# Mixing the last rows of a relational basis on VectorE, with interleaved one-hots

## The reference

```
w = jnp.einsum('rb,bio->rio', att, basis)      # att (2, 30), basis (30, 512, 512)
...
msg = jnp.where((edge_type == 0)[:, None], msgs[0], msgs[1])
agg = jax.ops.segment_sum(msg, row, num_segments=x.shape[0])
```

## Time and profile before

| | us |
|---|---|
| median of three runs | 918.7 |
| the three runs | 917.99, 918.7, 922.83 |
| the profiled execution, its own time | 917.2 |
| span of its trace | 915.4 |
| TensorE busy | 882.8 (96%) |
| VectorE busy | 656.2 (72%) |
| ScalarE busy | 280.8 (31%) |
| mean granted clock of TensorE | 0.985 |

### The profile page before, as it was taken

How to read it: one execution, slowest core, us unless ns; L and a number is a source line. 1 busy time by engine, 2 the same in 40 slices (tenths; PEclk the granted TensorE clock), 3 DMA queues, 4 the chain that set the end, 5 groups by cost and what they waited for, 6 DMA issues and landing times.

```text
span 915.4 us, 12673 instructions
## 1 busy us (share of the span) xinstructions
PE 882.8 (96%) x4258; PEld 428.2 (47%) x4258; DVE 656.2 (72%) x1286; ACT 280.8 (31%) x431; POOL 87.9 (10%) x66
## 2 busy tenths in 40 slices
PE   7999999999959999899997999999999999999997
PEld 3555555554545444344443444444444444444443
DVE  6898978658987797998999988975324255552247
ACT  0333444637752116222312111114311221132221
POOL 1000111301220003021210000003200020020000
PEclk9999999999979999999998999999999999999999
DMA  8955665596435885788464655530131014322228
GB/s 275 352 168 165 183 188 191 149 238 198 155 95 157 200 236 150 208 207 204 128 150 108 155 141 161 139 91 1 35 81 23 12 47 139 82 62 41 47 60 237
DMA packets 134888, 129.50 MB, mean 141 GB/s; under 512 B 80687, under 2 KB 81156, under 8 KB 134826
## 3 DMA queue, kind: packets, MB, share of 16 engines
q10 hardware_dynamic: 96192, 60.25, 26.1%
q1 hardware_dynamic: 38634, 68.45, 24.9%
HBM read 97.80 MB, written 12.52 MB: 121 GB/s over the span
## 4 chain that ended last, share of the span: by engine, by line
PE 68%; DVE 15%; DMA 8%; ACT 4%; issue 2%; POOL 1%; DVEq 1%; ACTq 0%; SPq 0%
PE Dp L696 25%; PE Dp L666 24%; PE T L620 11%; PE Dp L572 6%; DVE acc L1262 4%; DMA stage<-in_basis 3%; DMA wst<-mixd 2%; DMA xr<-xres 2%; DVE Zraw L1373 1%; ACT W L1010 1%; DVE stt L1354 1%; ACT wst L863 1%; DVE w L1391 1%; PE T L666 1%; POOL Zraw L530 1%
## 5 line engine op out<-in xcount | busy, mean ns | idle before, releaser
L666 PE MATMUL Dp<-W,hT 128*128 128x512 f16 x792 | 175.7, 381 | 3.6 <-DMA hT<-S 3.6
L696 PE MATMUL Dp<-Zraw,A 128*128 128x512 f16 x800 | 173.0, 379 | 0.0
L1262 DVE SCALAR_TENSOR_TENSOR acc<-stage,att,acc 128x512 f32<-128x512 f32 x232 | 163.5, 770 | 4.3 <-DMA stage<-in_basis 4.3
L696 PE MATMUL Dp<-Zraw,AT 128*128 128x512 f16 x600 | 130.0, 379 | 0.0
L666 PEld LDWEIGHTS Dp<-W,hT 128*128 128x128 f16 x792 | 77.8, 98 | 96.6 <-DMA hT<-S 3.8
L696 PEld LDWEIGHTS Dp<-Zraw,A 128*128 128x128 f16 x800 | 78.2, 98 | 94.4
L696 PEld LDWEIGHTS Dp<-Zraw,AT 128*128 128x128 f16 x600 | 58.7, 98 | 70.8
L1140 DVE TENSOR_SCALAR Zraw<-hT,w 128x640 f16<-128x640 f16 (+1 forms) x209 | 85.9, 456 | 0.3
L1391 DVE SCALAR_TENSOR_TENSOR w<-Dp,aggc,S 128x512 f32<-128x512 f32 x40 | 29.9, 747 | 59.9 <-PE Dp L696 54.0
L962 ACT ACTIVATE Zraw<-Dp,zsc 128x512 f16<-128x512 f32 x46 | 29.4, 684 | 125.8 <-PE Dp L666 121.7
L620 PE MATMUL T<-stage,W 128*128 128x512 f32 x120 | 60.5, 627 | 5.5 <-DMA stage<-in_basis 5.5
(11 more groups left out here) (176 smaller groups left out, 950.4 us busy)
## 6 DMA issues: line engine op xcount, KB each, us to landing
stage<-in_basis SPq DMA_DIRECT2D x180, 256.0 KB, 2.9
Zraw<-in_basis SPq DMA_DIRECT2D x60, 256.0 KB, 3.1
xres<-w ACTq DMA_DIRECT2D x30, 256.0 KB, 2.3
xr<-xres ACTq DMA_DIRECT2D x30, 256.0 KB, 3.1
wst<-in_Wn ACTq DMA_DIRECT2D x4, 1024.0 KB, 5.6
wst<-in_Ws ACTq DMA_DIRECT2D x4, 1024.0 KB, 6.0
wst<-mixd ACTq DMA_DIRECT2D x4, 1024.0 KB, 6.0
wst<-in_root ACTq DMA_DIRECT2D x3, 1024.0 KB, 6.7
```

What stands on the lines that cost most here:

```text
L666: last = nc.tensor.matmul(dense_bank(u, t, m), turned[:, hp, k * P:(k + 1) * P], weights_of(u, m)[:, wp, k, :], start=(n == 0), stop=(n == ...
L696: last = nc.tensor.matmul(sum_bank(t), a[:, k, ds(t * P, P)], Z[:, r, h, k, :], start=(n == 0), stop=(n == count - 1))
L1262: last = v.scalar_tensor_tensor(part, stage[:, q, :], a, part, ALU.mult, ALU.add)
```

## The change

Seven of the eight groups stay on TensorE (`PE_GROUPS`), six of them spread over the 40 windows as 7, 7, 7, 7, 6, 6. The last 64 rows of both relations are mixed on VectorE: relation 0 on partitions 0 to 63, relation 1 on 64 to 127. For this the same 64 rows of each basis are loaded twice, once for each half, into two slots that lie in `bias`; the column of coefficients is `late_att`, the sum `late_sum` in `Zraw`. One such step, `late_mix`, stands at the end of each of the windows 8 to 37. On the SP queue the two loads of step b stand ahead of the matmul's loads of the same share, and wait until step b-2 is done (`l_done`).

The four low one-hots of a window are written interleaved: element 4k + c belongs to column k of chunk c. Their comparison takes a prepared table `iota_c` and four neighbouring values of `lo_h`, in place of a broadcast of one value along 128 columns. TensorE reads the stationary operand of these four chunks in steps of four elements.

```diff
-        GROUP_BLOCKS = [6, 6, 6, 6, 5, 5, 6]
+        GROUP_BLOCKS = [7, 7, 7, 7, 6, 6]
...
+            for r in range(REL):
+                sp.dma_start(late_att[r * 64:(r + 1) * 64, :], att1[2 + r:3 + r, :].broadcast_to([64, BASES])).then_inc(e_att, 16)
+
+            def load_late(b):
+
+                wait(sp, l_done, b - 1)
+                for r in range(REL):
+                    sp.dma_start(late_in[b % 2][r * 64:(r + 1) * 64, :],
+                                 basis1[PE_GROUPS, b // 2, b % 2 * 64:(b % 2 + 1) * 64, :]).then_inc(l_full[b % 2], 16)
+
+            at = PAIRS + 2 * NT
+            for b in range(BASES):
+                nxt = PAIRS + 2 * NT + (PAIRS * PE_GROUPS - PAIRS - 2 * NT) * (b + 1) // BASES
+                load_late(b)
+                load_mix(at, nxt)
+                at = nxt
+            sp.wait_ge(l_done, BASES)
...
+            pool.iota(iota_c, [[1, P], [0, 2 * FIXED]], base=0, channel_multiplier=0, **kw).then_inc(s_const, 1)
...
+                if isinstance(slot, int):
+                    n = 2 * FIXED
+                    four = slot // n * n
+                    low = oh_lo[:, four * P:(four + n) * P].rearrange("p (k c) -> p k c", c=n)[:, :, slot % n]
+                else:
+                    low = oh_lo[:, ds(slot * P, P)]
...
+            def late_out():
+
+                act.wait_ge(l_done, BASES)
+                for r in range(REL):
+                    act.dma_start(mixd[r, PE_GROUPS * 64:GROUPS * 64, :],
+                                  late_sum[r * 64:(r + 1) * 64, :]).then_inc(s_mxst[PE_GROUPS % 2], 16)
...
-                v.tensor_tensor(oh_lo[:, slot * P:(slot + n) * P].rearrange("p (c k) -> p c k", c=n),
-                                iota_n[:, 0:P].rearrange("p (c k) -> p c k", c=1).broadcast_to([P, n, P]),
-                                lo_h[:, ds(c, n)].rearrange("p (c k) -> p c k", k=1).broadcast_to([P, n, P]), ALU.is_equal)
+                v.tensor_tensor(oh_lo[:, slot * P:(slot + n) * P].rearrange("p (k c) -> p k c", c=n),
+                                iota_c.rearrange("p (k c) -> p k c", c=n),
+                                lo_h[:, ds(c, n)].rearrange("p (k c) -> p k c", k=1).broadcast_to([P, P, n]), ALU.is_equal)
+
+            def late_mix(b):
+
+                if b == 0:
+                    dve.wait_ge(e_att, 64)
+                dve.wait_ge(l_full[b % 2], 16 * REL * (b // 2 + 1))
+                if b:
+                    dve.wait_ge(l_done, b)
+                    ins = v.scalar_tensor_tensor(late_sum, late_in[b % 2], late_att[:, b:b + 1], late_sum, ALU.mult, ALU.add)
+                else:
+                    ins = v.tensor_scalar(late_sum, late_in[0], late_att[:, 0:1], None, ALU.mult)
+                ins.then_inc(l_done, 1)
...
+                    if 0 <= w - LATE_FROM < BASES:
+                        late_mix(w - LATE_FROM)
```

More of the change, by code:

```diff
@@ L27 @@
 GROUPS = 2 * KT
+PE_GROUPS = GROUPS - 1
+LATE_FROM = 8
 MIX_SLOTS = 8
@@ L148, in resnorm_gnn_kernel @@
         dstr = hview(4 * 2 * P).bitcast(i32).rearrange("p (g e) -> p g e", g=2)
+        iota_c = dstr.bitcast(f16).rearrange("p g e -> p (g e)")
         wlo = hview(4 * NWIN).bitcast(f32)
@@ L164, in resnorm_gnn_kernel @@
         mix_in = [stage[:, q, :] for q in range(KT)] + [zview(4 * D).bitcast(f32) for _ in range(MIX_SLOTS - KT)]
+        late_att = att[:, 0, :]
+        late_in = [bias[:, i, :] for i in range(2)]
+        late_sum = zview(4 * D).bitcast(f32)
         W2 = W[:, 2, :, :, :].rearrange("p h k d -> p (h k d)")
@@ L224, in resnorm_gnn_kernel @@
         e_att = sem("e_att")
-        s_eye, s_mixT = sem("s_eye"), sem("s_mixT")
+        s_mixT = sem("s_mixT")
         mx_full = [sem(f"mx_full{i}") for i in range(MIX_SLOTS)]
@@ L228, in resnorm_gnn_kernel @@
         s_mxe = sem("s_mxe")
+        l_full = [sem(f"l_full{i}") for i in range(2)]
+        l_done = sem("l_done")
         s_mxst = [sem(f"s_mxst{i}") for i in range(2)]
@@ L265, in resnorm_gnn_kernel @@
         s_xst = {u: [sem(f"s_xst{u}_{j}") for j in range(2)] for u in LN}
-        b_idf, b_one, b_dg, b_row, b_rev = (sem("b_" + n) for n in ("idf", "one", "dg", "row", "rev"))
+        b_dg, b_row, b_rev = (sem("b_" + n) for n in ( "dg", "row", "rev"))
         b_ev, b_st, b_mv, b_sd, b_co, b_g = (sem("b_" + n) for n in ("ev", "st", "mv", "sd", "co", "g"))
@@ L289, in resnorm_gnn_kernel @@
         DG = Dp[:, 1, 2, 0:2 * NT]
-        GROUP_BLOCKS = [6, 6, 6, 6, 5, 5, 6]
-        assert sum(GROUP_BLOCKS) == NWIN and len(GROUP_BLOCKS) == GROUPS - 1
+        GROUP_BLOCKS = [7, 7, 7, 7, 6, 6]
+        assert sum(GROUP_BLOCKS) == NWIN and len(GROUP_BLOCKS) == PE_GROUPS - 1
         SHARES = [(i + 1) * PAIRS // n - i * PAIRS // n for n in GROUP_BLOCKS for i in range(n)]
@@ L431, in resnorm_gnn_kernel @@
         XS_FROM = 19
-        Z_SCALED = 38
+        Z_SCALED = 39
         def halves_split(u):
@@ L515, in _ @@
             pool.partition_all_reduce(rngr, rng, P, RMAX).then_inc(s_rngr, 1)
+            pool.iota(iota_c, [[1, P], [0, 2 * FIXED]], base=0, channel_multiplier=0, **kw).then_inc(s_const, 1)
             pool.memset(epsc[:, :], EPS).then_inc(s_const, 1)
             pool.memset(onec[:, :], 1.0).then_inc(s_const, 1)
-            pool.memset(ones, 1.0).then_inc(b_one, 1)
+            pool.memset(ones, 1.0).then_inc(s_const, 1)
             def reduce_weights(u):
@@ L569, in chunk_product @@
             def chunk_product(slot, j, start=False, stop=False):
+                if isinstance(slot, int):
[4 more added lines that the diff above has]
+                    low = oh_lo[:, ds(slot * P, P)]
                 for b in range(2):
-                    last = nc.tensor.matmul(Dp[:, j, b, 0:HALF], oh_lo[:, ds(slot * P, P)],
+                    last = nc.tensor.matmul(Dp[:, j, b, 0:HALF], low,
                                             oh_key[:, ds(slot * KEYS + b * HALF, HALF)], start=start, stop=stop)
@@ L624, in _ @@
             mix(PAIRS)
-            pe.wait_ge(s_const, 10)
+            pe.wait_ge(s_const, 11)
             pe.wait_ge(s_tbl, 1)
@@ L636, in _ @@
                 mix(mix_share(w))
-            assert mixed[0] == PAIRS * GROUPS
+            assert mixed[0] == PAIRS * PE_GROUPS
             pe.wait_ge(s_ate, 5 * (NT - 1))
-            pe.wait_ge(s_mxe, GROUPS)
+            pe.wait_ge(s_mxe, PE_GROUPS)
             for u, unit in enumerate(UNITS):
@@ L701, in spread @@
                 def spread():
-                    pe.wait_ge(b_one, 1)
+                    pe.wait_ge(s_const, 12)
                     for t in range(NT):
@@ L869, in load_bias @@
             def load_bias(u):
+                if u == 1:
+                    act.wait_ge(l_done, BASES)
                 if u > 2:
@@ L903, in _ @@
                 weight_work("counts", 0, t)
-            act.wait_ge(s_const, 10)
+            late_out()
+            act.wait_ge(s_const, 11)
             nc.scalar.activation(sd[:, 0:1], epsc[:, :], ACT.Sqrt)
@@ L1087, in _ @@
             dve.wait_ge(s_const, 8)
-            v.tensor_tensor(eye, ident[:, 0:P // 2], ident[:, P // 2:P], ALU.add).then_inc(s_eye, 1)
-            dve.wait_ge(s_eye, 1)
+            link(v.tensor_tensor(eye, ident[:, 0:P // 2], ident[:, P // 2:P], ALU.add))
             def mix_table(a0, a1):
@@ L1135, in _ @@
             dve.wait_ge(s_tbl, 1)
-            dve.wait_ge(s_const, 8)
+            dve.wait_ge(s_const, 9)
             def key_of(w, slot, c):
@@ L1314, in _ @@
                 dve.wait_ge(s_mxst[j], 16 * REL * GROUPS // 2)
-            v.tensor_copy(identf, ident[:, :]).then_inc(b_idf, 1)
-            dve.wait_ge(b_idf, 1)
+            link(v.tensor_copy(identf, ident[:, :]))
             for t in range(NT):
@@ L1544 @@
     lay["basis1"] = lay["basis1"].reshape(PAIRS, 2, GROUPS, 64, D).transpose(2, 0, 1, 3, 4).reshape(GROUPS, PAIRS, P, D)
-    lay["att1"] = lay["att1"].reshape(REL, PAIRS, 2).transpose(2, 1, 0).reshape(2, BASES)
+    lay["att1"] = np.concatenate([lay["att1"].reshape(REL, PAIRS, 2).transpose(2, 1, 0).reshape(2, BASES), lay["att1"]])
     for n in ("b0", "gamma", "beta"):
```

3 lines of the change are left out of this document (1 added, 2 removed).

## The result

The changed kernel takes **946.81 us** (median of four runs, 945.54 to 953.91) against 919.24 us for the kernel before, measured beside it on one chip (917.99 to 922.83): 27.6 us slower by the medians. The ratio on record is 1.0329, with a 95% interval of 1.0304 to 1.0355; it isn't the quotient of the two medians (1.0300), and 0.0329 of the time before is 30 us. So a difference that is told as a share of these 3.3% can come out up to 3 us larger than by medians, and where the two differ, both are given. The forecast was 923.7 us with a range of 916 to 930. The direction held, the size didn't: 5 us were forecast, 28 came.

What follows compares the result with a forecast made beforehand. TensorE ends the counts, with VectorE as full and only 3.5 us ahead at window 26. Terms 0 (counts) + 4.5 (loads) + 0.5 (behind the counts) = +5.0 us on the median 918.7 give 923.7 us, range 916 to 930.

Steps and rivals of the forecast that it cites:

- the loads of the new steps: Counts, steps 18 to 24: a loop of two windows from mixing matmul through load to products costs 4.5 us, at most 7.
- GpSimd's table: Start of the kernel: written by about 11 us, first read at 15 us, so no cost.
- Stretch 1: Counts up to VectorE's window 9: the first step ends near 47.8 us and VectorE gains 0.7 us.
- Stretch 2: VectorE's windows 9 to 25: 6.8 us more work; TensorE starts window 26 1.7 us later.
- Stretch 3: Window 26 to the end of the counts: TensorE ends them at 0, with -1.7 us as the lower end.
- last sentence on its signs: Counts: if the granted clock falls because TensorE has gaps, the cost is larger than any other term; no size given.
- Behind the counts: After the counts: ScalarE's two more stores ahead of its table load cost 0 to 0.6 us, taken as 0.5.
- strided weights: TensorE's products in the counts: stationary operands loaded in steps of four elements cost nothing, at most 0.43 us per window.
- The first: Rival, counts: the loads arrive in time, without the 4.5 us; -1.7 to +2 us, 917 to 921 us; chance 0.16.
- The second: Rival, counts: TensorE stays the bound and VectorE's stretch is elastic; at least 5 us gained, 906 to 914 us; chance 0.11.
- The third: Rival, VectorE in the counts: the one-hots do not get shorter; 8.4 us on top, 932 us; chance 0.08.
- the fourth: Rival, TensorE in the counts: the strided weights are slow; some +8 us, 927 us; chance 0.07.

Runs made afterwards that it cites:

- e1: The changed kernel with GpSimd's table iota_c written ahead of its all-reduce instead of behind it; 945.9 us, ratio 1.0300 to the kernel before.
- e5: The kernel before with the interleaved one-hots alone, GpSimd's table iota_c written ahead of the all-reduce; 920.68 us, ratio 1.0027.
- e8: The kernel before with the interleaved low one-hots alone, their table written by ScalarE; 916.68 us, ratio 0.9986.
- e3: The changed kernel with the steps in windows 10 to 39 instead of 8 to 37; 921.33 us, ratio 1.0046 to the kernel before.
- e9: The changed kernel with the steps in windows 10 to 39 and the table written by ScalarE; 917.00 us, ratio 0.9999 to the kernel before.
- e6: The changed kernel without the interleaved one-hots and their table, the 30 steps alone in windows 8 to 37; 945.63 us, ratio 1.0294 to the kernel before.
- e13: The changed kernel with each load one place earlier on SP's queue, table by ScalarE, GpSimd's first weights behind the last one-hots; 920.45 us, ratio 1.0031.
- e11: As e10, but 22 steps in windows 18 to 39 and the last 8 behind the counts, from eight slots of their own; 918.23 us, ratio 1.0000.
- e10: As e9, but GpSimd waits for VectorE's last one-hots before it subtracts the first weights; 914.37 us, ratio 0.9956 to the kernel before.
- e2: The changed kernel with only the first two half bases loaded, all 30 steps still done; 927.38 us, ratio 1.0113 to the kernel before.
- e12: The changed kernel with each step's pair of loads one place earlier on SP's queue; 926.05 us, ratio 1.0095 to the kernel before.
- e7: The changed kernel, loading only 16 of 512 columns of each half basis from the third base on; 936.43 us, ratio 1.0211 to the kernel before.

## Why the prediction was wrong

The step that failed is the term for the loads of the new steps: 4.5 us, at most 7, and 18 to 21 measured. A second step that failed is GpSimd's table, put at nothing, and a third the work of GpSimd beside VectorE, which the forecast saw at window 26 and didn't price where the new steps end.

**Stretch 1: wrong by GpSimd's table.** "GpSimd's table is written by about 11 us and first read at 15 us" failed: it was written at 19.3 us and held VectorE for 6.4. I had costed the new instruction by its length (1.19 us) and not by what stood between it and its neighbour, though the trace of before had a gap of that kind, 6.79 us of "issue" ahead of the same all-reduce (a part of which is the wait for VectorE's result: in e1 that wait lets the numbering go at 7.12 us). Worth 3.8 to 4.3 us by the ratios (e5 to e8, e3 to e9), 4.5 and 2.5 at window 39 in the traces. That it is hidden behind the loads in the changed kernel itself is argued: e6, which took as long, has neither the table nor the shorter one-hots.

**Stretch 2: right once the rest is taken away.** The steps took 0.66 us from start to start as forecast (164.68 to 165.52 is one with a wait in it), 797 ns busy on average. The low one-hots came down from 713 to 476 ns, 0.24 us for each against 0.27. The forecast had TensorE's window 26 1.7 us later; e13, which has the loads in time but for the first and no late table, has it 2.3 us later (126.8 for 124.5), the changed kernel 13.3. Here is e13's first step:

```profile
47.37 0.48 DVE L1214 TENSOR_SCALAR Zraw<-bias,att 128x512 f32<-128x512 f32 x1 [1.73 <-DMA bias<-in_basis]
```

It ended at 47.85 us, where the forecast had 47.8. But the next one-hots began 0.59 us behind it, at 48.44, so the 0.7 us that stretch 1 was to gain came to nothing; that is the difference of 2.3 to 1.7. The balance of 9.5 us off TensorE against 6.8 on VectorE was sound. What it left out is where VectorE had no lead even before: in windows 8 to 13 it also takes the maxima of x, the piece ahead of 75.09 us in the earlier trace rows. Steps there delay TensorE at once: window 14 starts at 72.7 us in e11, which has none before window 18, at 74.6 in e10 and at 77.3 in e13. Of e13 and e10, which differ in the begin of the steps and the loads' place relative to them, the second is 0.75% better, 6.9 us. The traces place 2.7 us of it ahead of window 13 (68.95 to 66.25), where e13 has two steps more and the wait of 1.73 us, and 2.0 between windows 28 and 32 (18.5 to 16.5), where both do the same work and e13's TensorE, with less lead to cover keys that are slow beside GpSimd, waits. So the windows 8 and 9 alone are not the whole of it, and what steps and load each take of the 2.7 is open.

**Stretch 3: a right size with a term missing.** Between windows 26 and 39 the kernel before takes 54.8 us, e13 54.2 and e10 52.2, within the forecast's 0 to 3.4 less. The 1.57 us beside GpSimd that I had in the rows came back larger, in window 39, where VectorE now works when GpSimd begins on the weights: e9 to e10, 0.43%, 3.9 us.

**The loads of the new steps: the mis-sized term.** The mechanism was named, a loop of two windows from mixing matmul to load to step to keys to products, and the price was 4.5 us with an upper end of 7. It measured 18 to 20 (e2) or 18 to 21 us (e12), by medians and by ratios. Three things made the difference. I gave the loop 5.1 us from the first mixing matmul to the start of the window but one; in TensorE's rows from 158.56 to 166.94 us it took 8.4: 1.1 for the matmul itself, which I left out, 0.9 for the issues (0.4), 4.1 to the landing (3.0) and 2.3 for step and keys (1.7). I let it act for b from 18 to 24 alone; VectorE waited for loads from its first step (1.04 us), and the chain has a load at 48.70, 91.05, 108.85, 138.09, 147.42, 160.56, 173.45 and 185.34 us. Of what the changed kernel is behind e12 in the table, 9.2 us stand at window 26, where the forecast had put nothing, and 13.6 more come by window 39. And the longer waits of TensorE cost again through its clock. The granted clock (ahead of the DMA share, the columns as in the first fence) in stretches of 4 us, behind two waits of TensorE of 3.3 us (to 80.86) and 3.6 us (to 101.51):

```profile
80.00:84.00 4.00, 3.14 (x16) 1.83 (x17) 3.66 (x11) 0.27 (x1) 0.00 (x0) 0.50 0.52 189
84.00:88.00 4.00, 4.00 (x22) 2.12 (x20) 3.66 (x11) 0.92 (x2) 0.00 (x0) 0.67 0.37 91
88.00:92.00 4.00, 4.00 (x25) 2.57 (x23) 4.00 (x12) 1.19 (x2) 0.00 (x0) 1.00 0.56 154
100.00:104.00 4.00, 2.49 (x10) 1.46 (x11) 3.91 (x10) 0.00 (x0) 0.00 (x0) 0.53 0.28 85
```

At 0.50, 1.2 GHz, ten products take 2.83 us instead of 1.36, and the mixing that releases the next pair is late too. The forecast's last sentence on its signs named this and gave it no number.

**Behind the counts.** 0.5 us were forecast, 29.0 - 29.15 = -0.15 came: nothing. The **strided weights** cost nothing, as forecast: their loads take 116 ns instead of 98, still under the products, and ten products take 1.36 us in the chain. The Trainium skill's note on cachelines (SBUF — State Buffer, Door 1), by which a step of 8 bytes is still at full rate, holds here for the time and not for the loads themselves: in e5, whose stretch from 130 to 140 us has no wait for VectorE or a slower clock, they take 114 ns, 16 more than packed ones.

**The rivals.** The first, that the loads arrive in time, gave 917 to 921 us; e12, where they do and nothing else is changed, took 926.05 and e2 927.38, above it by the table and GpSimd's weights; e13, without these, took 920.45. The second (TensorE stays the bound, faster) needed VectorE to be elastic. It was not: e10 gets faster by other orders and a later begin, and even there TensorE waits 3.30 us for the keys of window 14. The third and the fourth are out. Set against 1.0329, by the ratios, the loads' place takes 2.3% (21 us), GpSimd's table and its weights together 0.64% (6 us, e12 to e13), and 0.31% (3 us) is left, where the forecast's other terms came to 0.5 us with 2 as the upper end.

## What to carry to other kernels

When a step is put on an engine ahead of the work that feeds the bound, and its data come by a queue whose entries wait for that bound, write out the whole circle, with the releasing instruction itself, every issue, the longest landing seen and the work up to the bound's next start, and place the load one turn earlier than the sum asks for; here one place in the queue was worth 18 to 21 us. Begin such steps where the engine has lead in every window, not on average (without steps ahead of window 18, e11 starts window 26 3.1 us earlier than e10). And cost a new instruction by its neighbours too: a change of kind on GpSimd, or work of GpSimd beside VectorE's, was worth more here than the instruction.

## What the runs showed of the hardware

- GpSimd stood still for 7.05 to 7.81 us between a numbering and an all-reduce over partitions, in either order (7.57 in the changed kernel, 7.05 in e3, 7.75 in e1, 7.81 in e5), and for 6 to 7 us ahead of the all-reduce even where none of the new instructions was there (6.79 before, 6.07 in e8), which includes its wait for VectorE's result. Why it does was not tested.
- In the changed kernel waits of TensorE of 3.3 and 3.6 us were followed by a granted clock of 0.50 and 0.53, which was 0.67 and 0.61 in the next stretch of 4 us and 1.00 in the one behind it. Behind shorter waits it fell in some places (0.71 from 156 us on, behind 2.6 us) and in others not (1.00 from 180 us on, behind 1.8 us).
- VectorE's f16 one-hots went from 0.80 us for two keys to 3.46 beside GpSimd's subtraction of f32 and f16, while the new f32 step took 1.60 us at the longest in the changed kernel (0.75 in the middle).
- The interleaved low one-hots took 0.42 us in some windows and 0.56 in others, with the same shape. They were the same windows in e8 and e10 (6 to 11, 16 to 19, 25, 30, 31 and 37 to 39 took 0.54 to 0.56), so it goes with the window and not with the new steps, which e8 doesn't have; the start of the four values in `lo_h` is a candidate that was not tested.
- Loads of 128 KB landed in 2.4 to 6.5 us, 3.5 in the middle, no sooner than 256 KB (3.3 and 3.7 in the middle); those of 4 KB in e7 took 2.4 in the middle.
